# A later generator, own banks for the second tile, another order in the last steps, and seventeen idle matmuls

## The reference

```python
scale = cond @ norm_w.T + 1.0
h = x * (scale[:, None, :] * jax.lax.rsqrt(ms + EPS))      # ms: mean of x*x over a row
val, gate = jnp.split(h @ up_w.T, 2, axis=-1)              # 1024 columns each
h = val * jax.nn.gelu(gate, approximate=False)
y = act_quant(h) @ weight_quant(down_w).T + x              # x is now this
dWd = ((cond @ Wdd.T + bdd) * 0.1).reshape(B, 128, 256)    # dWu likewise
down = relu(x @ (Wd + dWd).T + bd)
out = x + down @ (Wu + dWu).T + bu
```

## Time and profile before

| | |
|---|---|
| median of 3 runs | 480.67 us (480.03 to 480.86) |
| the profiled execution | 480.89 us, of which the span is 479.2 us |
| busy: TensorE, VectorE, ScalarE, GpSimd | 97%, 79%, 76%, 54% of the span |
| chain that ended last | TensorE 88%, VectorE 5%, ScalarE 3% |
| largest groups on the chain | `up` (L1022) 64%, `down` (L1036) 11% |

### The profile page before, as it was taken

One profiled execution on the slowest core, in us unless ns is written; L12 is line 12 of the kernel. 1 busy time (PEld: TensorE's weight loads), 2 busy tenths in 40 slices (PEclk: granted clock), 3 DMA queues, 4 the chain that ended last, 5 costly groups with the idle time before them and its releaser, 6 DMA issues.

```text
span 479.2 us, 10039 instructions
## 1 busy us (share of the span) xinstructions
PE 467.1 (97%) x3278; PEld 271.3 (57%) x3278; DVE 377.8 (79%) x789; ACT 365.5 (76%) x636; POOL 260.2 (54%) x676
## 2 busy tenths in 40 slices
PE   8989999999999999999999999999999999999995
PEld 7445656666565455555555555555555555555563
DVE  4798988898898787877877788786777877777776
ACT  5889999999997678768676876867776777777662
POOL 0295775657655446475573746557374543444653
PEclk9999999999999999999999999999999999999997
DMA  7957787777873455565554466455445544544332
GB/s 269 349 113 205 180 244 227 189 210 181 253 176 89 92 121 100 137 147 117 148 133 107 128 141 155 111 153 126 103 136 133 143 103 119 130 123 90 72 85 89
DMA packets 117860, 71.01 MB, mean 148 GB/s; under 512 B 102000, under 2 KB 102960, under 8 KB 115632
## 3 DMA queue, kind: packets, MB, share of 16 engines
q1 hardware_dynamic: 117648, 70.29, 57.2%
q10 hardware_dynamic: 160, 0.07, 0.1%
HBM read 37.44 MB, written 8.39 MB: 96 GB/s over the span
## 4 chain that ended last, share of the span: by engine, by line
PE 88%; DVE 5%; ACT 3%; issue 2%; DMA 1%; POOL 0%; DVEq 0%; ACTq 0%; SPq 0%; POOLq 0%
PE bank L1022 64%; PE bank L1036 11%; PE bank L1113 4%; PE bank L1127 4%; PE bank L1095 4%; PE bank L993 1%; DVE adapt L716 1%; ACT gel L552 1%; DVE xs_lo L746 1%; DMA qT<-qn 1%; DVE hid L767 1%; DVE amax L775 1%; ACT tern L650 0%; ACT qn L574 0%; DVE x L879 0%
## 5 line engine op out<-in xcount | busy, mean ns | idle before, releaser
L767 DVE SCALAR_TENSOR_TENSOR hid<-bank,rms,gel 128x512 f32<-128x512 f32 x127 | 95.2, 750 | 80.4 <-ACT gel L552 79.4
L552 ACT ACTIVATE gel<-bank,rms 128x512 f32<-128x512 f32 x127 | 86.9, 684 | 90.7 <-PE bank L1022 90.6
L1022 PE MATMUL bank<-up_hi,xs_hi 128*128 128x512 f16 x508 | 151.2, 379 | 3.0 <-DVE hid L767 1.5
L1022 PE MATMUL bank<-up_lo,xs_hi 128*128 128x512 f16 x508 | 151.1, 379 | 0.7 <-DVE up_lo L931 0.7
L1022 PE MATMUL bank<-up_hi,xs_lo 128*128 128x512 f16 x508 | 151.1, 379 | 0.0
L1022 PEld LDWEIGHTS bank<-up_lo,xs_hi 128*128 128x128 f16 x508 | 49.6, 98 | 60.9 <-DVE up_lo L931 1.4
L1022 PEld LDWEIGHTS bank<-up_hi,xs_lo 128*128 128x128 f16 x508 | 49.7, 98 | 59.9
L775 DVE TENSOR_REDUCE amax<-hid 128x1 f32<-128x1024 f32 x63 | 76.9, 1220 | 2.2
L565 ACT ACTIVATE hid<-hid,amax 128x1024 f32<-128x1024 f32 x64 | 72.4, 1132 | 2.3 <-DVE amax L781 1.8
L403 POOL TENSOR_TENSOR wsplit<-stage,wsplit 128x288 f16<-128x288 f32 x64 | 52.8, 853 | 34.9 <-ACT wsplit L527 34.9
L1022 PEld LDWEIGHTS bank<-up_hi,xs_hi 128*128 128x128 f16 x508 | 48.3, 98 | 38.5 <-DVE xs_lo L746 2.9
(11 more groups left out here) (129 smaller groups left out, 633.3 us busy)
## 6 DMA issues: line engine op xcount, KB each, us to landing
xT_s<-in_xT SPq DMA_DIRECT2D x32, 256.0 KB, 3.0
xn_s<-in_xn SPq DMA_DIRECT2D x32, 256.0 KB, 3.1
stage<-in_WddT SPq DMA_DIRECT2D x8, 1024.0 KB, 5.4
stage<-in_WduT SPq DMA_DIRECT2D x8, 1024.0 KB, 5.2
out<-out_s SPq DMA_DIRECT2D x31, 256.0 KB, 2.4
adapt<-in_up_wT SPq DMA_DIRECT2D x4, 512.0 KB, 6.8
x<-in_down_wT SPq DMA_DIRECT2D x1, 1024.0 KB, 10.0
qT<-qn SPq DMA_TRANSPOSE x63, 3.1
```

The costliest lines, as they stand in the source:

```text
L552: nc.scalar.activation(gel[:, c], u_gate[c][:], ACT.Gelu, scale=rms[:, t // TPB % XN_SLOTS, t % TPB:t % TPB + 1]).then_inc(gelu_done, 1)
L767: nc.vector.scalar_tensor_tensor(out=hid[:, t % 2, c * 512:(c + 1) * 512], in0=u_val[c][:], scalar=rms[:, t // TPB % XN_SLOTS, t % TPB:t % ...
L1022: ins = nc.tensor.matmul(dst[:], a[:, t // TPB % 2, k, cols], w[:, c, k, v, :], start=(k == 0 and n == 0), stop=(k == KD - 1 and n == 2))
```

## The change

The generator (`chunk`) and the adapter steps begin one step later. The loads are put in another order: the up weights ahead of xn, the down weights in two halves, the adapter's base weights ahead of the first chunk. The roots of sequences 0 and 1 are begun behind the splitting of the up weights, that of sequence 2 moves from step 2 to step 3. Tile 1 gets the banks 4 to 7 and waits for no bank (`u_banks(t, c)` picks them, for `up`, `gelu` and `gate`). The sum of the down weights is taken in two halves and its matmuls stand in step 2; the ternary passes are spread over step 2. down(0) and down(1) both stand in step 4, residual(0) in step 4, residual(1) and residual(2) in step 5. Behind the loop `q_transpose` goes ahead of down(62), middle(30) ahead of two x_transposes; ScalarE, VectorE and GpSimd get a matching order, and GpSimd's last output bias (now one half at a time, `output_bias_last(i)`) waits for residual_low of the last tiles. Two of nine `idle` matmuls go, and `fill` adds 5 + 3 + 3 + 6 matmuls of 256 columns, whose results nobody reads.

```diff
-N_SMALL = 6
+N_BASE = 4
+N_SMALL = 2
...
-IDLE_SECOND = 9
+IDLE_SECOND = 7
+FILL_SUMS = 5
+FILL_HALVES = 3
+FILL_MIDDLE = 3
+FILL_OUTPUT = 6
...
-    return max(2 * b + 7, NGEN + 5 + (4 * b + 2) // 3)
+    return max(2 * b + 7, NGEN + 6 + (4 * b + 2) // 3)
...
 def scales(s):
-    return [b for b in range(1, B) if max(2 * b - 2, 1) == s]
+    return [b for b in range(2, B) if max(2 * b - 2, 3) == s]
+def downs(s, c):
+    late = {(4, 0): [0], (4, 1): [1]}
+    return late.get((s, c), [s - DOWN] if c == 0 and s - DOWN >= 2 else [])
+def residuals(s):
+    return {4: [0], 5: [1, 2]}.get(s, [s - DOWN] if s - DOWN > 2 else [])
 def chunk(s, lag):
-    return [s - 2 - lag] if 0 <= s - 2 - lag < NGEN else []
+    return [s - 3 - lag] if 0 <= s - 3 - lag < NGEN else []
...
-        sum_ps = y_ps[:, 0:1]
+        sum_ps = bank[5][:, 0:1]
+        second_val = [bank[5], bank[7]]
+        second_gate = [bank[6], bank[4]]
...
             sp.dma_start(cond2[0:C, :], condT).then_inc(ld_cond, 16)
-            load_x(0)
+            sp.dma_start(xT_s[:, 0], xT[0]).then_inc(ld_xT[0], 16)
             for n in range(NC * KD):
                 sp.dma_start(raw_up[:, n // KD, n % KD], up_wT[:, n // KD, n % KD]).then_inc(ld_up[n], 16)
-            load_x(1)
-            sp.dma_start(raw_down, down_wT).then_inc(ld_down, 16)
+            for b in range(2):
+                sp.dma_start(xn_s[:, b], xn[b]).then_inc(ld_xn[b], 16)
+            for i in range(2):
+                part = slice(i * JF * D // 2, (i + 1) * JF * D // 2)
+                sp.dma_start(raw_down[:, part], down_wT[:, part]).then_inc(ld_down[i], 16)
+                if i == 0:
+                    sp.dma_start(xT_s[:, 1], xT[1]).then_inc(ld_xT[1], 16)
+            for i, (w, b) in enumerate(((WdT, bddT), (WuT, bduT))):
+                sp.dma_start(base[:, i, :], w).then_inc(ld_base, 16)
+                sp.dma_start(bias_raw[:, i, :], b).then_inc(ld_base, 16)
+            load_x(2)
             load_chunk(0)
-            load_x(2)
-            for i, (w, b) in enumerate(((WdT, bddT), (WuT, bduT))):
-                sp.dma_start(base[:, i, :], w).then_inc(ld_small, 16)
-                sp.dma_start(bias_raw[:, i, :], b).then_inc(ld_small, 16)
             sp.dma_start(bd_col[:], bd).then_inc(ld_small, 16)
             sp.dma_start(bu_row[:], bu.to_broadcast([P, D])).then_inc(ld_small, 16)
             load_chunk(1)
...
@@ -494,8 +523,7 @@
                 for q in chunk(s, 0):
                     low_part(q)
                 for b in scales(s):
-                    if b > 1:
-                        rsqrt(b)
+                    rsqrt(b)
                 if s == LAST_T - 1:
                     residual_low(LAST_T - 4)
                 for b in adapter_splits(s):
@@ -508,10 +536,13 @@
             middle_low(B - 4)
             dequantization(LAST_T)
             residual_low(LAST_T - 2)
+            output_bias(B - 2)
             middle_low(B - 3)
-            output_bias(B - 2)
+            pool.wait_ge(x1_lo_done, LAST_T - 2)
+            output_bias_last(1)
             middle_low(B - 2)
-            output_bias_last()
+            output_bias_last(0)
...
@@ -632,23 +663,30 @@
...
+            def absolute_sum(i):
+                part = slice(i * JF * D // 2, (i + 1) * JF * D // 2)
+                act.wait_ge(ld_down[i], 16)
+                nc.scalar.activation(tern[:].rearrange("p j d -> p (j d)")[:, part], raw_down[:, part], ACT.Abs,
+                                     accum_out=wsum[:, 3 * i:3 * i + 1]).then_inc(absum_ready, 1)
             scaled_high(0)
-            squares(0)
             for n in range(NC * KD):
                 act.wait_ge(ld_up[n], 16)
                 nc.scalar.activation(up_part(up_hi, n // KD, n % KD), raw_up[:, n // KD, n % KD], ACT.Copy, scale=U_SCALE
                                      ).then_inc(up_hi_ready, 1)
+            squares(0)
+            squares(1)
+            absolute_sum(0)
             for s in range(NT):
                 for b in sequences(s, -1):
                     relu(b)
                 gelu(s, 0)
                 if s == 0:
+                    gelu(0, 1)
                     scaled_high(1)
-                    squares(1)
-                    gelu(0, 1)
-                    act.wait_ge(ld_down, 16)
-                    nc.scalar.activation(tern[:].rearrange("p j d -> p (j d)"), raw_down, ACT.Abs,
-                                         accum_out=wsum[:, 0:1]).then_inc(absum_ready, 1)
+                if s == 1:
+                    absolute_sum(1)
+                    gelu(1, 1)
                 if s >= 1:
                     quantize(s - 1)
                 if s < LAST_T:
@@ -658,22 +696,21 @@
                     gelu_piece(0)
                 if s >= 1:
                     quantized(s - 1)
-                if 0 < s < LAST_T:
+                if 1 < s < LAST_T:
                     gelu(s, 1)
                 for q in chunk(s, 0):
                     high_part(q)
                 if s % TPB == 0 and 1 < s // TPB + 1 < B:
                     scaled_high(s // TPB + 1)
                 for b in scales(s + 1):
-                    if b > 1:
-                        squares(b)
+                    squares(b)
             gelu_piece(1)
             residual_high(LAST_T - 3)
             relu(B - 4)
             quantize(LAST_T)
             quantized(LAST_T)
+            residual_high(LAST_T - 2)
             qT_evacuate()
-            residual_high(LAST_T - 2)
             relu(B - 3)
             residual_high(LAST_T - 1)
             x61_evacuate()
...
@@ -923,26 +960,23 @@
...
             scaled_low(0)
-            rsqrt_guess(0)
-            rsqrt_first()
             for n in range(NC * KD):
                 c, k = n // KD, n % KD
                 dve.wait_ge(up_hi_ready, n + 1)
                 nc.vector.scalar_tensor_tensor(out=up_part(up_lo, c, k), in0=raw_up[:, c, k], scalar=U_SCALE,
                                                in1=up_part(up_hi, c, k), op0=ALU.mult, op1=ALU.subtract
                                                ).then_inc(up_ready, 1)
+            rsqrt_guess(0)
+            rsqrt_first()
+            rsqrt_guess(1)
             for s in range(NT):
                 if s == LAST_T:
                     total(B - 5)
                 gate(s, 0)
-                if s == 0:
-                    scaled_low(1)
-                    rsqrt_guess(1)
                 if s == 2:
-                    ternary_second()
-                    ternary_third()
-                if s >= DOWN:
-                    residual(s - DOWN)
+                    ternary_first()
+                for t in residuals(s):
+                    residual(t)
                 if s < LAST_T:
                     for b in sequences(s, -2):
                         total(b)
@@ -952,15 +986,18 @@
                 if s % TPB == 1 and 1 < s // TPB + 1 < B:
                     scaled_low(s // TPB + 1)
                 for b in scales(s):
-                    if b > 1:
-                        rsqrt_guess(b)
+                    rsqrt_guess(b)
                 for b in adapter_splits(s):
                     adapter_high(b)
                 if s < LAST_T:
                     gate(s, 1)
+                    if s == 0:
+                        scaled_low(1)
+                    if s == 2:
+                        ternary_second()
                     quant_scale(s)
-                    if s == 1:
-                        ternary_first()
+                    if s == 2:
+                        ternary_third()
                     for t in split_tiles(s):
                         if t < LAST_T - 4:
                             residual_low(t)
@@ -972,6 +1009,7 @@
             gate_piece(1)
             quantize_last()
             residual(LAST_T - 2)
+            total(B - 4)
             qT_evacuate()
             residual(LAST_T - 1)
             residual(LAST_T)
@@ -980,7 +1018,6 @@
             residual_low(LAST_T - 1)
             x63_lo_evacuate()
             x62_evacuate()
-            total(B - 4)
             total(B - 3)
             split_last()
             total(B - 2)
...
@@ -1006,8 +1043,10 @@
             def up(t, c):
-                after(pe, gelu_done, (t - 1) * NC + c + 1)
-                after(pe, hid_done, (t - 1) * NC + c + 1)
+                held = 0 if t == 2 else t - 1
+                if t != 1:
+                    after(pe, gelu_done, held * NC + c + 1)
+                    after(pe, hid_done, held * NC + c + 1)
                 cols = slice(t % TPB * P, (t % TPB + 1) * P)
                 for k in range(KD):
                     passes = ((xs_hi, up_hi), (xs_lo, up_hi), (xs_hi, up_lo))
...
@@ -1073,6 +1112,10 @@
                         ins = nc.tensor.matmul(y_ps[:, 0:D], qT[:, LAST_T % QT_SLOTS, f], tern[:, f],
                                                start=(f == 0), stop=(f == JF - 1))
                 ins.then_inc(y_full, 1)
+            def fill(dst, n):
```

(30 more changed lines are left out.)

16 lines of the change are left out of this document (7 added, 9 removed).

## The result

The changed kernel takes 484.90 us (median of five executions, 483.94 to 485.20), the kernel before 480.67 (480.03 to 482.00): ratio 1.0082, 95% interval 1.0067 to 1.0098. It is slower by 4.2 us; 484.3 had been predicted. The profiled execution took 484.90 us, with a span of 483.2.

What follows compares the result with a forecast made beforehand. TensorE's matmul sum was taken to bound the middle, with start and tail changes carried to the end one for one. Median 480.67 + 5.0 start + 1.7 clock - 3.1 tail = 484.3 us; range 481.8 to 487.0.

Steps and rivals of the forecast that it cites:

- the 4.8 forecast: Start, before down(1): TensorE idles 4.8 us until residual(0), which the late root of sequence 2 holds back, ends at 44.6.
- Start, without the clock: Steps up to up(20,0): waits before down(1) and down(2) make the start +5.0 us, bounds +4.2 and +5.8.
- The 1.5 us for `gate`: Kernel before, before 70 us: TensorE's longest waits, given as 1.5 us for `gate`.
- The clock: TensorE's granted clock falls in the wait before down(1), slowing down(1), generate(0), up(5,0): +1.7 us, bounds 0 and 3.4.
- a stretch at half clock as long as the one at 470.5, 3.4 us: After the wait before down(1): half clock lasts 3.4 us, as in the kernel before's tail, and half is lost.
- Rival A: Start: the wait before down(1) comes but the clock holds over it, 482.6 us; chance 0.20.
- rival B: Clock falls twice in the start, or in the tail in spite of the fills, 486.0 us; chance 0.13.
- Rival C: Start: root of sequence 2 in time, down(1) and down(2) never wait, start -1.9, 475.7 us; chance 0.12.
- the banks of up(5,0) free: Start: up(5,0), its banks free, would not pass the waiting down(1); if it could, the 2.1 us would be gone.
- The tail: Last steps: earlier q_transpose, shorter residual_low and middle(30) moved ahead together give -3.1 us.
- the pair of residual_low: Tail: residual_low(63) and (62) no longer run beside GpSimd's output_bias(31), -0.9 us.
- What they buy is the clock: Tail: the seventeen fill matmuls hold the clock; if it falls anyway, the tail gives only -1.5 us.

Runs made afterwards that it cites:

- experiment 1: Changed kernel with GpSimd making the root of sequence 2 before the low part of chunk 0 in step 3: 477.97 us, ratio 0.9943.
- experiment 9: Changed kernel with the squares, guess and root of sequence 2 back in steps 1 and 2, as in the kernel before: 478.99 us, ratio 0.9959.
- experiment 5: Changed kernel with the root of sequence 2 ahead of GpSimd's low part and residual(1) moved behind gate(4,1): 475.31 us, ratio 0.9889.
- experiment 2: Changed kernel with 44 unused matmuls of 256 columns between up(4,1) and down(1): 484.67 us, ratio 1.0065.
- experiment 4: Changed kernel without its seventeen fill matmuls, new orders kept: 484.25 us, ratio 1.0064.
- experiment 12: Changed kernel with root of sequence 2 first, residual(1) behind gate(4,1), third ternary pass in step 3, no fill matmuls: 474.37 us, ratio 0.9871.

## Why the prediction came out right, and where its terms were off

Place and order of every link were as predicted, and each link after the root of sequence 0 came a little early: that root 0.1 us, high_part(0) at 35.6 (36.5), the root of sequence 2 at 41.9 (42.7), residual(0) at 43.8 (44.6). Experiments 1 and 9 show that the root behind the low part makes the wait of 5.3 us, experiment 5 shows that residual(1) behind gate(5,0) makes that of 2.1. The wait is longer than the 4.8 forecast because TensorE came early as well (38.7, not 39.8): up(4,0) waited 2.06 us for xs_lo(2), not 3.4.

**Start, without the clock.** Predicted +4.7 at up(6,0) and +5.0 (4.2 to 5.8) at up(20,0). Less the clock's 2.4 us the trace has 6.75 - 2.4 = +4.35 and 6.96 - 2.4 = +4.56. The 0.4 us are the early links. (The 1.5 us for `gate` that the prediction calls the longest wait before 70 us are two waits, the longer 1.0; nothing rests on it.)

**The clock.** Predicted +1.7, measured 2.4 (experiment 2 at its place). The term that was mis-sized is "a stretch at half clock as long as the one at 470.5, 3.4 us": in this execution the granted clock was low from 42.3 to 49.1, 6.8 us, of which TensorE worked the 5.1 from 43.96. Half of that is 2.6. In the profile of experiment 4, behind the same wait, the forecast 3.4 us came out, all of them busy, so 1.7 us were lost there. The stretch is thus not one length, and the prediction gave it one.

The two errors have opposite signs: 6.7 us were predicted for both at up(20,0), and 6.96 were seen. That the sum came out so near is luck in part. Rival A (the clock holds, 482.6) did not happen in the profiled execution, and none of the five had a mean clock above 0.996 (0.989 to 0.996); a second fall, rival B, is not in the profile, and of the other four executions only the mean is known. Rival C failed at its own mark, since residual(0) ended at 43.8 and not by 42.7.

The prediction has the banks of up(5,0) free while TensorE stood before down(1). They were not until gate(4,0) ended, at 43.42. generate(0) is the better case: its low parts were there at 38.75, and still it started behind down(1). No matmul starts between 38.7 and 43.96. That is the rule cited in the prediction, that matmuls stay in program order (the Trainium skill, TensorE: Matmul & The Clock Gate, Part 2), and this trace agrees.

**The tail.** Predicted -3.1, measured -3.1 by the traces (17.0 to 13.8 us). Shifted by 7.1, the prediction's times were 472.4 for down_last, 475.25 for the end of residual_low(62) and 480.5 for the end of the last total; the trace has 472.49, 475.24 and 480.55. That the pair of residual_low would lose its 0.9 us once GpSimd's output_bias is elsewhere was right, though it is the bias of sequence 30 and not 31, as the prediction has it. In the kernel before the two bars last 0.83 and 0.94 us, and each ends 0.29 us behind one of GpSimd's (468.33 and 469.19); here they take 0.38 each. The Trainium skill (SBUF — State Buffer, SBUF: two separate sides) says that of the port pair which VectorE and GpSimd share one instruction has all and the other stands still, and these times agree.

What failed in the tail is "What they buy is the clock": without the fills the clock held where it was seen (the profile of experiment 4, all four executions of experiment 12), and the tail was 0.5 to 0.6 us shorter. It changed nothing in the sum, which had the fills' cost in it.

**What stays open.** Why the clock fell behind some waits of about 2 us and not behind others: three of six executions of experiment 1 and four of seven of experiment 9 lost it, though each time the program is the same; where they lost it is seen only in the one with a profile. Nor why it stayed low for 6.8 us behind one wait of 5.3 and for 3.4 behind the other. No run here tells what decides.

## What to carry over

On an engine that works in program order, look at what stands ahead of the small operation that others wait for: here twelve tiny operations of GpSimd behind a low part that nobody needed yet cost 5.3 us and a clock, and moving one call gave 6.9 us back. When a step is moved by one, walk every queue that it passes, since its neighbours (the root, residual(1)) may have been in time only by the old distance. A wait of TensorE costs more than its length where the clock falls behind it; the profile's one execution shows one case of it, so look at the mean clock of all of them.
